# Score pass of a two-layer graph network: the loads of the upper block issued two steps later in the sync queue

## The reference

```
D = |x[:, :, None, :] - x[:, None, :, :]|
h = D @ W1.T + b1;  h = batch-normalised over all pairs, * g1 + be1
s = leaky(h) @ W2.T + b2            # one score for each pair
s = where(adj > 0, s, NEG);  A = softmax(s)
y = (A @ x) @ Wg.T + bg;  y = leaky(normalised y)
out = concat(x, y) @ Wt.T + bt;  x = layernorm(x + out)
```

## Time and profile before

| | us |
|---|---|
| median of 3 runs | 2385.34 (2384.91 to 2387.01) |
| the profiled execution | 2389.64 |
| its span, first to last instruction | 2387.4 |
| busy in it: ACT, DVE, PE | 2169.8, 2125.1, 1997.7 |

### The profile page before, as it was taken

The page is one execution under the profiler, slowest core; times in us unless marked ns, Lnnn a source line. Parts: engine busy times, 40 slices in busy tenths (PEclk is TensorE's granted clock), DMA queues, the critical chain, the costliest instruction groups (busy, mean ns, idle before and its releaser), DMA issues.

```text
span 2387.4 us, 35023 instructions
## 1 busy us (share of the span) xinstructions
PE 1997.7 (84%) x12741; PEld 793.2 (33%) x12741; DVE 2125.1 (89%) x2647; ACT 2169.8 (91%) x2988; POOL 47.1 (2%) x50
## 2 busy tenths in 40 slices
PE   5777767888888888888888888888789899989876
PEld 4555543333332323333232323232222222222226
DVE  5888868999999999999999999999899999999866
ACT  5999977999999999999999999998799999999875
POOL 0000000000000000000000000000000000000000
PEclk8999989999999999999999999999899999999997
DMA  4111105444444444444444444443799899989862
GB/s 119 41 41 41 41 18 168 172 178 173 172 174 174 173 178 168 177 169 175 174 172 177 174 176 175 175 176 159 303 355 356 342 350 351 352 344 355 336 256 71
DMA packets 221280, 470.49 MB, mean 197 GB/s; under 512 B 52344, under 2 KB 143288, under 8 KB 196536
## 3 DMA queue, kind: packets, MB, share of 16 engines
q1 hardware_dynamic: 220048, 467.91, 51.8%
q10 hardware_dynamic: 1064, 0.36, 0.1%
HBM read 254.25 MB, written 213.91 MB: 196 GB/s over the span
## 4 chain that ended last, share of the span: by engine, by line
ACT 33%; PE 21%; issue 17%; DVE 16%; DMA 9%; SPq 4%; ACTq 0%; POOLq 0%; POOL 0%; DVEq 0%
PE banks L870 10%; ACT diff L613 7%; DVE diff L1213 6%; ACT hcopy L625 5%; ACT yt L630 5%; ACT habs L625 5%; DMA ring_scores<-sring 4%; DVE ring L1085 4%; ACT habs L657 3%; PE banks L784 3%; DMA hcopy<-kept 2%; PE banks L955 2%; DVE diff L1227 2%; DMA diff<-kept 2%; ACT diff L657 2%
## 5 line engine op out<-in xcount | busy, mean ns | idle before, releaser
L870 PE MATMUL banks<-diff,w1t 128*64 128x512 f32 x5136 | 1213.0, 603 | 171.1 <-DVE diff L1227 56.2
L1213 DVE TENSOR_TENSOR diff<-ring 128x2048 f32<-128x2048 f32 x352 | 802.9, 2289 | 93.4 <-PE banks L870 93.4
L870 PEld LDWEIGHTS banks<-diff,w1t 128*64 128x64 f32 x5136 | 341.0, 137 | 913.5 <-issue 822.4
L1227 DVE TENSOR_SCALAR diff<-diff 128x2048 int32<-128x2048 int32 x354 | 415.6, 1221 | 0.0
L1342 DVE TENSOR_TENSOR diff<-ring 128x2048 f32<-128x2048 f32 x128 | 292.5, 2285 | 19.0 <-PE banks L870 18.9
L613 ACT ACTIVATE diff<-banks 128x2048 f32<-128x2048 f32 x128 | 238.5, 1863 | 1.3 <-PE banks L885 1.3
L625 ACT ACTIVATE hcopy<-banks 128x1024 f32<-128x1024 f32 x192 | 194.2, 1019 | 26.4 <-PE banks L870 26.4
L625 ACT ACTIVATE habs<-banks 128x1024 f32<-128x1024 f32 x192 | 194.1, 1019 | 25.8 <-PE banks L870 25.8
L955 PE MATMUL banks<-habs,w2s 128*32 128x512 f32 x816 | 159.2, 601 | 56.7 <-ACT hcopy L657 24.5
L630 ACT ACTIVATE yt<-hcopy,par 128x2048 f32<-128x2048 f32 x96 | 192.5, 2005 | 3.1
L630 ACT ACTIVATE yt<-habs,par 128x2048 f32<-128x2048 f32 x96 | 192.5, 2005 | 3.1
(11 more groups left out here) (215 smaller groups left out, 1933.5 us busy)
## 6 DMA issues: line engine op xcount, KB each, us to landing
kept<-hcopy SPq DMA_DIRECT2D x192, 512.0 KB, 2.8
kept<-habs SPq DMA_DIRECT2D x192, 512.0 KB, 2.8
hcopy<-kept SPq DMA_DIRECT2D x78, 1024.0 KB, 8.3
diff<-kept SPq DMA_DIRECT2D x76, 1024.0 KB, 8.3
habs<-kept SPq DMA_DIRECT2D x38, 1024.0 KB, 8.4
yt<-xrows SPq DMA_DIRECT2D x512, 40.0 KB, 2.0
adjt<-in_adj_dram SPq DMA_DIRECT2D x32, 256.0 KB, 2.8
diff<-in_x_dram SPq DMA_DIRECT2D x32, 128.0 KB, 2.1
```

What stands on the lines that cost most here:

```text
L870: last = nc.tensor.matmul(dst[half * O:(half + 1) * O, bank * BANK:(bank + 1) * BANK], w1t[:, :], src[:, m * BANK:(m + 1) * BANK], start=T ...
L1213: v.tensor_tensor(shaped(diff[:, c % ND, :]), xj, xi_, ALU.subtract).then_inc(sub_done, 1)
L1227: v.tensor_scalar(bits, bits, ABS_BITS, None, ALU.bitwise_and).then_inc(abs_dve, 1)
```

## The change

One condition in SP's loop: `load_blocks(b - 2)` is called at step 4 instead of step 2.

```
                 if kk == 7 and 1 <= b <= B:
                     store_scores(b - 1)
-                if kk == 2 and 2 <= b <= B + 1:
+                if kk == 4 and 2 <= b <= B + 1:
                     load_blocks(b - 2)
```

## The result

The changed kernel takes 2412.78 us (median; 2407.96 to 2421.7), the kernel before 2385.21 us beside it: ratio 1.0118, 95% interval 1.0088 to 1.0148. It is about 28 us slower, where 10 us faster was forecast. The profiled execution has a span of 2410.3 us, 22.9 more than before.

The account below looks back on a forecast made before the run. It took ACT's work plus late unit loads as the bound. A period of 10.4 + 9.07 = 19.5 us instead of 19.83 saves 0.33 us, times 30 gives 10 us: 2375 us from 2385.34, range 2357 to 2397.

Parts of the forecast that it names:

- What bounds the kernel: Score pass: ACT's work plus the lateness of unit loads, 0.9 us of waits in a 19.83 us period.
- SP's queue after the change: SP's load queue: units three and four issued at t0 + 0.1 and + 0.6, blocks from + 1.2 to + 5.7.
- ACT's waits for units "taken as gone": ACT in the score pass: all its waits for kept data units vanish, 0.9 us a period.
- Landing of the blocks, t0 + 9.0: Block loads: land 1.3 us after the second of two units, which is down at t0 + 7.7.
- t0: Score pass: moment PE frees the buffers of units three and four, as the matmuls of L870 begin.
- The mask, 1.33 us by its mean: POOL's mask after the blocks land: takes 1.33 us before PE may transpose the blocks at L965.
- the forecast's + 10.4: PE at L965: masked blocks ready at t0 + 10.4, with bounds t0 + 8.7 and t0 + 11.9.
- PE's stall at L965, 1.5 us: PE at L965: waits 1.5 us a period for the masked blocks, a wait absent before.
- From L965 to the next t0, 9.07 us: PE's work from L965 to the next buffer release: 9.07 us, its idle time for ACT gone.
- 19.47 us forecast: Score pass period: 10.4 + 9.07, given as 19.5 us against 19.83 before.
- The slower rival: PE's stall at L965: queue backlog remains at t0, period 21.0 us, 35 us slower, 2420; chance 0.26.
- B: Theory of the follow-up experiments, not the prediction: POOL's mask is held up by DVE, so PE's stall has two sizes.

Follow-up runs that it names:

- behind one unit, no POOL: Kernel before with block loads one step later, behind one unit load, POOL's mask left out, PE and DVE waiting for the loads themselves: 2372.12 us, ratio 0.9933.
- behind one unit: Kernel before with the block loads one step later, not two, so behind one unit load, mask still on POOL: 2375.6 us, ratio 0.9949.
- Without POOL: Changed kernel with POOL's mask left out, PE and DVE waiting for the block loads themselves: 2380.28 us, ratio 0.9979.

## Why the prediction was wrong

- **What bounds the kernel: right.** Unit loads were late because the block loads, with their wait for the stored scores, stood ahead of them; moved by one unit instead of two, they give 12 to 13 us.
- **SP's queue after the change: right**, within 0.2 us.
- **ACT's waits for units "taken as gone": wrong.** 9.5 us in 240 stayed. PE's longer stall frees the buffers later, so the loads begin later as well; but in the kernel where PE has no stall 4.3 us remain too (behind one unit, no POOL).
- **Landing of the blocks, t0 + 9.0: a step that failed.** On the mean of 25 periods (t0 from 1761.55 to 2277.34) it was + 9.95, so 0.95 too early in the forecast. In the first of the two periods above the first unit landed 5.3 us after its issue, as into an empty queue, the second 8.2 us after its issue at 2091.47, so at t0 + 8.7 instead of + 7.7, and the blocks followed by 1.7, where I had taken 1.3 from a queue that was running dry. In the other period the second unit landed at t0 + 7.7, as forecast, and the blocks 1.8 later. Why the two periods differ in the second unit is not shown.

```profile
habs<-kept SPq DMA_DIRECT2D x1, 1024.0 KB, 5.3
diff<-kept SPq DMA_DIRECT2D x1, 1024.0 KB, 8.2
```

- **The mask, 1.33 us by its mean: the wrong kind of term.** I took the mean of a group of 30 as the cost of an instruction. It is two things: 0.7 us of work, and the rest of whatever DVE is running. With the landings of this kernel it ends at t0 + 10.28 or + 11.54, and hardly ever between. As a mean it was not too small: it measured 1.03 over the 25 periods. That the forecast's + 10.4 holds for the better half of the periods is luck: there the landing was 0.5 too early and the mask 0.5 too long. The rows before show the hold-up: L1347 at 2059.11 took 1.64 us beside the mask. There it cost nothing, since PE had 1.9 to 3.4 us in hand.
- **PE's stall at L965, 1.5 us: thus too small.** L965 started at t0 + 11.03 on the mean instead of + 10.4, a stall of some 2.1 to 2.2 us.
- **The clock: missing from the sum, the other step that failed.** A stall of PE was priced at its length. Where the clock falls behind it, it costs 1.64 us more; over the 25 periods 0.8 us a period, some 22 us in the pass.
- **From L965 to the next t0, 9.07 us: 0.3 too much** where the clock holds (8.8). With this, a period with the short stall is 10.34 + 8.78 = 19.12 us; 12 of the 25 periods are of that kind (19.12 to 19.27), the other 13 take 20.38 us or more.
- **The sum, put right:** 19.47 us forecast, + 0.95 for the landing, - 0.3 for the mask, - 0.3 for the way from L965 to t0, + 0.8 for the clock, gives the measured 20.63 within rounding.
- **The slower rival** had the right place and point (L965, from t0 + 10.8 on), but not the cause: it wanted a queue not yet drained at t0, and the first unit landed after 5.3 and 4.8 us in the two periods shown. Of 0.8 us a period: the short stall alone would have made the period 0.7 us faster; the longer stall in half of the periods gives back 0.7, the clock 0.8 on the mean.

On B, the Trainium skill, "SBUF — State Buffer", section "SBUF: two separate sides", states that DVE and GpSimd (POOL) share a pair of ports to the on-chip memory SBUF as an exclusive lock, that a DVE instruction in a two-port mode, or one with two SBUF inputs against a GpSimd one that reads SBUF, takes part in it, and that whichever starts first has the pair for its whole instruction while the other blocks. The runs agree: an instruction of POOL on two elements took 0.20 or 1.06 us, one that began 0.14 us into L1342 (two inputs) ended after it, and L1347, begun 0.02 us after a mask, took 0.55 us longer. L1347 has one input; that it runs in a two-port mode is not shown by any run. This rule spoke against the change, and I did not weigh it.

## What to carry to other kernels

Before moving a transfer behind another one, follow it to the engine that uses it, and ask at each instruction on the way what else can hold it: here POOL, which is almost idle, was a link of 0.7 us or of 2.7, depending on what DVE ran. Price a new stall of PE with its consequence for the clock, and read a "mean ns" that differs from the shortest instance as a sign of two cases. In this queue the small urgent transfers did best one place behind the large ones (0.9949), not two (1.0118) or three (1.051): the optimum lay between the two kernels, and a run for each place costs little.

## What the runs showed of the hardware

- A POOL mask that began while DVE ran its subtraction (2.28 us) or its absolute value (1.23 us) ended only 0.54 to 0.59 us after that DVE instruction. The DVE instruction that began meanwhile was longer by up to 0.55 us (L1347 1.63 to 1.78 for 1.23; L1342, behind one unit, 2.83 for 2.28).
- The granted TensorE clock fell from 2.4 to 1.2 GHz after ten of the twelve stalls of 2.71 or 2.72 us in the pass of the changed kernel, and not after the other two: at 2042.68 the stall was 2.72 us too, and the four matmuls behind it took 1.03 us, the full-speed time. After its stalls of 1.46 to 1.61 us it did not fall. Without POOL it fell once after a stall of 1.96 us, and not after one of 2.35. So the length of the stall alone doesn't decide; what does is not shown.

```profile
2042.68 0.55 PE L965 MATMUL banks<-ident,ub 128*128 128x128 f32 x3 [2.72 <-POOL ub L514]
2043.07 1.03 PE L990 MATMUL banks<-probt,yt 128*128 128x256 f32 x4
```

- The DMA engines moved 363 GB/s over 240 us (behind one unit, no POOL). The limit of about 358 GB/s from HBM for each core, which the Trainium skill gives on "DMA: Bandwidth & Descriptors", section "Specifications", was no ceiling for this one core.
